# Turning quantised weights by DMA instead of on TensorE, in a one-core kernel of FFN, GRU and experts

## The chip, the cores and the metric

One core of a Trainium2 chip. The metric is the device time of one execution of the program in microseconds, as the median of several runs. The engines are PE (TensorE), DVE (VectorE), ACT (ScalarE), POOL (GpSimd) and SP (SyncE, which here only issues DMAs). Each runs its own instructions in order and waits for the others through semaphores.

## What is computed

```python
x = x + ffn0(cond0(x))        # x: 16 x 256 x 512, f32
x = x + experts1(gru1(x))

def ffn0(x):                  # microscaled ("MX") blocks of 32 along the last axis
    gate = q_act(x) @ q_w(w_gate).T        # w_gate, w_up: 2048 x 512
    up   = q_act(x) @ q_w(w_up).T
    return q_act(silu(gate) * up) @ q_w(w_down).T      # w_down: 512 x 2048

def q_w(w):                   # per block of 32: a shared power of two, then 1 mantissa bit, clipped at 6
    scale = 2 ** (floor(log2(max|w|)) - 2)
    return quantize_elem(w / scale, 2, 1.0, 6.0) * scale
```

cond0 sums blocks of 16 steps (x to 16 sums per batch row), forms keys, a softmax over the sums and a projection, adds it to x and normalises. gru1 is a GRU over the 256 steps, experts1 a linear layer with two of 16 low-rank experts per row. Only q_w of the three FFN weights, and where its result is put, is touched by the change.

## The kernel before

x is cut into 32 tiles of 128 rows (8 steps of 16 batch rows). A software pipeline goes over the tiles in slots, `slot(c, s)` with s from 0 to 7, one GRU step in each; FFN, GRU input products, GRU and experts work on different tiles in one slot. All but the first 170 us or so is this pipeline, and PE sets its pace.

Before it stands the weight stage. The three FFN weights are 24 pieces of 128 x 1024 f32 (512 KB). Each goes through five hands:
- SP loads it to `wst[u]`, u = p % 2 (L318; the second buffer is named `sg_gs` in the profile). It waits on `w_y` until POOL has scaled piece p-2 out of that buffer.
- DVE takes block maxima and makes scales from them (`scales`, L577 to L585), three pieces ahead of the rounding. The scales of piece k wait on `w_out` until piece k-4 is multiplied.
- POOL multiplies by the inverse scale (`scale_piece`, L989, output `gi`).
- ACT computes `absolute` (L420) and `summand` (L427), from which DVE rounds in two steps (L593, L595).
- POOL multiplies back (`piece`, L1002) into `wqn[u]`, bf16, which lies in `qfT`. It waits on `w_mm` until PE has turned piece p-2 out of that buffer.
- PE turns the piece in 8 blocks of 128 x 128 to PSUM (`ps_gate_up` or `ps_z`, L1083), and ACT copies it to its place in `wq` (`keep_piece`, L414).

POOL's order is scale 0, scale 1, then for each p: scale p+2, multiply back p. ACT's order for each p: keep p-1, absolute p+2, summand p+1. PE's order for each p: `block_sums(p)`, a step of `attention`, turn p. SP's order for each p: load p, then `beside(p)`: two or three of the 32 x tiles of 256 KB (until p = 12, in a ring of 8, each waits on `summed` for the tile 8 before), two small constants (p = 8 to 14), WkT and WoT (p = 13 and 15), chunks of W_hh (p = 18 to 21), the slots of c = -4 (from p = 21). The 10 steps of the attention (block sums to `proj`) stand one to a piece from p = 11 on, on every engine. From p = 21 on the slots of c = -4 stand between the pieces: `xs` (L1013), its statistics and normalisation.

After the last piece DVE takes maxima of W_hh (`chunk_max`, L698), PE turns them to a row (L1320), and the first FFN product (L1131) follows it.

Of the kernel before, what the change touches and what calls it, by code (L numbers as in the profile page):

```python
# [24 lines left out]
BF16 = mybir.dt.bfloat16  # L25
# [9 lines left out]
P = 128  # L35
# [19 lines left out]
PIECE = 1024  # L55
# [11 lines left out]
ROUND_UNIT = 2.0 ** 3  # L67
MOST_ROUND = (ROUND_UNIT * (255 + ROUND_LEAST)) ** 2
W_CLIP = 3.0
SCALED = 2.0 ** 13  # L70
LEAST = 2.0 ** -40
FILLS = 7
# [11 lines left out]
def wait(engine, sem, value):  # L84

    if value > 0:
        engine.wait_ge(sem, value)
# [11 lines left out]
def build(nc, x_steps, h0, ident, pick, block_mask, iota, rms_w, query, WkT, WoT, gamma, beta,  # L99
          ffn_w, W_ih, W_hh, b_ih, b_hh, WL, bias, rb1, rw2T, rb2, gates, BT, x1_dram, out):  # L100
    with ExitStack() as ctx:
# [3 lines left out]
        def sem(name):  # L105
            return ctx.enter_context(nc.semaphore(name))
# [133 lines left out]
        w_loaded = [sem(f"w_piece_loaded{u}") for u in range(2)]  # L240
        w_small, w_y, w_abs_ok = sem("w_scales"), sem("w_scaled"), sem("w_absolute")
        w_round_ok, w_added = sem("w_rounding_ready"), sem("w_rounding_added")
        w_q, w_out, w_mm, w_ev = sem("w_rounded"), sem("w_quantised"), sem("w_turned"), sem("w_kept")
        c_dve = sem("consts_computed")

        xin_loaded, xs_done, q_stat, ve_done, rstd_done = (
# [35 lines left out]
        def count_piece(turn, u, more=0):  # L282

            return turn * 2 + (u + more)
# [27 lines left out]
        @block.sync  # L312
        def _(sp):

            def piece(turn, u):
                wait(sp, w_y, count_piece(turn, u, -1))
                at = (turn * 2 + u) * P
                sp.dma_start(wst[u][:, :], ffn_w[at:at + P, :]).then_inc(w_loaded[u], 16)  # L318

            small = [(rw_b, rms_w.partition_broadcast(P)), (q_b, query.partition_broadcast(P)),  # L320
                     (maskA[:, :], block_mask), (iota_b[:, :], iota.partition_broadcast(P)),
                     (gamma_b[:, :], gamma.partition_broadcast(P)), (beta_b[:, :], beta.partition_broadcast(P)),
                     (bias_b[:, :], bias.partition_broadcast(P)), (b_i[:, :], b_ih), (b_h[:, :], b_hh),
                     (rb1_b[:, :], rb1.partition_broadcast(P)), (rb2_b[:, :], rb2[0:EXPERTS].partition_broadcast(P)),
                     (gates_b[:, :], gates.partition_broadcast(P)), (rw2_sb[:, :], rw2T)]
            assert len(small) == CONSTS

            def x_upto(p):

                if p < 0:  # L330
                    return 0
                return min(TILES, max(min(p + 1, 2) * XRING // 2, (p - 1) * TILES // SUM_PARTS))

            def beside(p):

                for t in range(x_upto(p - 1), x_upto(p)):
                    wait(sp, summed, t - XRING + 1)
                    sp.dma_start(xtile[t % XRING], x_steps[t * P:(t + 1) * P, :]).then_inc(xt_loaded[t % XRING], 16)
                if 8 <= p < 8 + (CONSTS + 1) // 2:
                    for dst, src in small[(p - 8) * 2:(p - 7) * 2]:  # L340
                        sp.dma_start(dst, src).then_inc(consts if p > 8 else att_consts, 16)
                if p == SUM_PARTS + 1:
                    sp.dma_start(wk_sb, WkT).then_inc(wkwo_loaded, 16)
                if p == SUM_PARTS + 3:
                    sp.dma_start(wo_sb, WoT).then_inc(wkwo_loaded, 16)
                    sp.dma_start(h[:, :], h0).then_inc(h0_loaded, 16)
                    load_x_in(0)
                k = p - FIRST_HOP - 7
                if 0 <= k < KD:
                    sp.wait_ge(at_pe, 2)  # L350
                    sp.dma_start(wih[:, k, :], W_hh[:, k, :]).then_inc(whh_loaded, 16)
                if p >= FIRST_SLOT:
                    slot(-4, p - FIRST_SLOT)

            def loads(c):
                Q, F, E, I, R, L = stages(c)
                if L:
                    wait(sp, x1b_done, count(c - 1, 1))
                    sp.wait_ge(x1_stored, count(c, 1) * 16)
                    sp.dma_start(x1_in[:, :], rows(x1_dram, c - 1)).then_inc(x1in_loaded, 16)  # L360
                if E:
                    wait(sp, x1_done, count(c + 2, 1))
                    sp.dma_start(xres[:, :], rows(x_steps, c + 2)).then_inc(xres_loaded, 16)

            def load_x_in(q):
                wait(sp, xs_done, count(q, 1))
                sp.dma_start(xin[:, :], rows(x_steps, q)).then_inc(xin_loaded, 16)

            def stores(c):
                Q, F, E, I, R, L = stages(c)  # L370
                if E:
                    sp.wait_ge(x1_done, count(c + 2, 1, 1))
                    sp.dma_start(rows(x1_dram, c + 2), x1[:, :]).then_inc(x1_stored, 16)
                if L:
                    sp.wait_ge(y_ok, count(c - 1, 1, 1))
                    sp.dma_start(rows(out, c - 1), y[:, :]).then_inc(y_stored, 16)

            def rows(dram, t):
                return dram[t * P:(t + 1) * P, :]

            def slot(c, s):
                if s == 0:
                    loads(c)
                if s == 4 and c + 5 < TILES:
                    load_x_in(c + 5)
                if c == -3 and s == STEPS - 2:
                    sp.dma_start(wl[:, 1:KD + 1, :], WL).then_inc(wl_loaded, 16)
                    for k in range(KD):
                        sp.wait_ge(whh_lo, min(k + 2, KD))
                        sp.dma_start(wih[:, k + 1, :], W_ih[:, k, :]).then_inc(wih_loaded, 16)  # L390
                    sp.dma_start(bt[:, :, :], BT).then_inc(bt_loaded, 16)
                if s == STEPS - 1:
                    stores(c)

            for p in range(PIECES):
                piece(p // 2, p % 2)
                beside(p)
            for s in range(PIECES - FIRST_SLOT, STEPS):
                slot(-4, s)
            over_tiles(slot)  # L400
            sp.wait_ge(y_stored, 16 * TILES)
            sp.wait_ge(x1_stored, 16 * TILES)
# [3 lines left out]
        def _(act):  # L406
            first = [(idf[:, :], ident), (pick_sb[:, 0:pick.shape[1]], pick)]
            for dst, src in first:
                act.dma_start(dst, src).then_inc(first_consts, 16)

            def keep_piece(turn, u):
                ps = (ps_up, ps_z)[u]
                act.wait_ge(w_mm, count_piece(turn, u, 1))
                nc.scalar.activation(wq[:, turn * 2 + u:turn * 2 + u + 1, :], ps[:, :].bitcast(BF16).unsqueeze(1),  # L414
                                     ACT.Copy).then_inc(w_ev, 1)

            def absolute(p):
                act.wait_ge(w_y, p + 1)
# [11 lines left out]
            def piece(turn, u):  # L430
                p = count_piece(turn, u)
                if p == 0:
                    absolute(0)
                    summand(0)
                    absolute(1)
                if p > 0:
                    keep_piece((p - 1) // 2, (p - 1) % 2)
                if p + 2 < PIECES:
                    absolute(p + 2)
                if p + 1 < PIECES:  # L440
                    summand(p + 1)
                if p == PIECES - 1:
                    keep_piece(turn, u)

            def attention(step):

# [519 lines left out]
        def _(pool):  # L966
# [25 lines left out]
            def piece(turn, u):  # L992

                p = count_piece(turn, u)
                if p + 2 < PIECES:
                    scale_piece(turn + 1, u)
                attention(p - FIRST_HOP)
                if p >= FIRST_SLOT:
                    slot(-4, p - FIRST_SLOT)
                pool.wait_ge(w_q, count_piece(turn, u, 1))  # L1000
                wait(pool, w_mm, count_piece(turn, u, -1))
                g.tensor_tensor(blocked(wqn[u]), blocked(wy[p % 3]), spread(wsc[p % 4][:, :]),  # L1002
                                ALU.mult).then_inc(w_out, 1)

# [60 lines left out]
        def _(pe):  # L1065
            mm, turn_ = nc.tensor.matmul, nc.tensor.transpose
            def block_sums(p):
# [3 lines left out]
                for t in range(p * TILES // SUM_PARTS, min((p + 1) * TILES // SUM_PARTS, TILES)):  # L1071
# [1 line left out]
                    first = (BLOCKS - 1 - t * BLOCKS // TILES) * B  # L1073
                    mm(ps_down[:, :], pick_sb[:, first:first + P], xtile[t % XRING], start=t == 0,
                       stop=t == TILES - 1).then_inc(summed, 1)

            def piece(turn, u):

                ps = (ps_up, ps_z)[u]
                wait(pe, w_ev, count_piece(turn, u, -1))  # L1080
                pe.wait_ge(w_out, count_piece(turn, u, 1))
                for m in range(PIECE // P):
                    last = turn_(ps[:, :].bitcast(BF16)[:, m * P:(m + 1) * P], wqn[u][:, m * P:(m + 1) * P], idb[:, :])  # L1083
                last.then_inc(w_mm, 1)

            def attention(step):
                if step == 1:
# [258 lines left out]
            for p in range(PIECES):  # L1346
                block_sums(p)
                attention(p - FIRST_HOP)
                piece(p // 2, p % 2)
            for s in range(STEPS):  # L1350
                slot(-4, s)
            pe.wait_ge(w_ev, PIECES)
            over_tiles(slot)


# [54 lines left out]
```

## Time and profile before

| | |
|---|---|
| time, median of 3 runs | 1749.04 us (1748.38 to 1749.63) |
| profiled execution | 1750.32 us, its span 1748.5 us |
| busy in the span | PE 1585.6 us (91%), DVE 1417.0 (81%), ACT 710.7 (41%), POOL 498.4 (29%) |
| DMA | 80.09 MB, mean 46 GB/s; 246, 265, 141, 111 GB/s in the first four of 40 slices |
| mean granted TensorE clock | 0.958 |

The span is from the first to the last instruction of the profiled execution. The table's shares are means over the whole span, and most of it is the pipeline; the weight stage is its first three slices (43.7 us each). So the views below are cut to the first 170 us. PE, DVE and so on are the engines' own busy time; "idle before <- releaser" is what an engine waited for before an instruction. Numbers like 1.00 under PEclk are the granted TensorE clock as a share of 2.4 GHz.

### The profile page before, as it was taken

How to read it: one execution, taken by the hardware profiler on the slowest of the kernel's cores; microseconds unless marked ns; L12 is line 12 of the kernel's file. 1: busy time of each engine (PE TensorE's matmuls, PEld its weight loads, DVE VectorE, ACT ScalarE, POOL GpSimd, SP SyncE). 2: the span in 40 equal slices, each digit the busy share in tenths (PEclk: the TensorE clock that was granted, in tenths of full speed). 3: DMA queues.
4: the chain of work that ended last, by engine and by line, in shares of the span. 5: the costliest groups of instructions: out<-in, count | busy, mean ns of one | idle time of the engine just before them, and what ended most of it. 6: DMA issues, size and time to landing. Idle time of an engine off the chain costs nothing.

```text
span 1748.5 us, 76340 instructions
## 1 busy us (share of the span) xinstructions
PE 1585.6 (91%) x32908; PEld 1240.8 (71%) x32908; DVE 1417.0 (81%) x5579; ACT 710.7 (41%) x1760; POOL 498.4 (29%) x573
## 2 busy tenths in 40 slices
PE   5534489999999999999999999999999999999986
PEld 2221167777787877778777777877777777778874
DVE  7898888888888888888888888888888888887654
ACT  5653244444444344434344434443443444443331
POOL 6773232222222222222222222222222222221100
PEclk9855699999999999999999999999999999999998
DMA  7733100011001010001111000110100010000000
GB/s 246 265 141 111 43 26 27 34 33 33 13 29 33 33 33 33 29 31 34 33 33 34 33 26 16 33 33 33 33 33 27 33 33 33 27 27 27 21 15 20
DMA packets 35408, 80.09 MB, mean 46 GB/s; under 512 B 4864, under 2 KB 5248, under 8 KB 34688
## 3 DMA queue, kind: packets, MB, share of 16 engines
q1 hardware_dynamic: 34784, 75.03, 12.6%
q8 instruction: 259, 4.24, 1.1%
q14 instruction: 77, 0.63, 0.1%
q10 hardware_dynamic: 288, 0.19, 0.0%
HBM read 58.43 MB, written 16.78 MB: 43 GB/s over the span
## 4 chain that ended last, share of the span: by engine, by line
PE 76%; DVE 16%; issue 2%; DMA 2%; POOL 2%; ACT 1%; DVEq 0%; ACTq 0%; POOLq 0%; SPq 0%
PE ps_rn_turn L1305 23%; PE ps_gi L1198 11%; PE ps_z L1305 10%; PE ps_gate_up L1137 6%; PE ps_down L1155 6%; PE ps_gate_up L1131 4%; PE ps_base L1207 4%; PE ps_base L1251 3%; PE ps_route L1207 3%; DVE fe L795 1%; PE ps_rn_turn L1146 1%; PE ps_rn_turn L1175 1%; DVE gi L595 1%; DVE gi L593 1%; DVE zn L780 1%
## 5 line engine op out<-in xcount | busy, mean ns | idle before, releaser
L1305 PE MATMUL ps_rn_turn<-hT,whh 128*128 128x32 f16 x16320 | 449.2, 176 | 39.2 <-DVE hT L733 38.8
L1305 PEld LDWEIGHTS ps_rn_turn<-hT,whh 128*128 128x128 f16 x16320 | 435.0, 96 | 65.7 <-DVE hT L733 58.2
L1020 POOL TENSOR_TENSOR qf<-f8c,fe 128x512 bf16<-128x512 bf16 x128 | 135.6, 1059 | 892.4 <-DVE f8c L812 872.8
L1198 PE MATMUL ps_gi<-x1T,wih 128*128 128x128 f16 x4608 | 288.6, 219 | 1.2 <-ACT gi L544 1.2
L1198 PEld LDWEIGHTS ps_gi<-x1T,wih 128*128 128x128 f16 x4608 | 270.3, 98 | 25.6 <-issue 1.5
L553 ACT ACTIVATE r_tanh<-r_pre,scale_half 128x64 f32<-128x64 f32 x256 | 89.0, 348 | 461.5 <-DVE r_pre L753 461.5
L1305 PE MATMUL ps_z<-hT,whh 128*128 128x32 f16 x8160 | 243.3, 176 | 0.0
L1305 PEld LDWEIGHTS ps_z<-hT,whh 128*128 128x128 f16 x8160 | 222.7, 96 | 0.0
L544 ACT ACTIVATE gi<-ps_gi,b_i,scale_x 128x128 f32<-128x128 f32 x384 | 144.7, 457 | 181.9 <-PE ps_gi L1198 181.9
L747 DVE TENSOR_TENSOR r_half<-ps_rn_turn,gi 128x64 f32<-128x64 f32 x256 | 56.6, 221 | 137.6 <-PE ps_rn_turn L1305 134.4
L555 ACT ACTIVATE z_tanh<-z_pre,scale_half 128x64 f32<-128x64 f32 x256 | 89.0, 348 | 157.9 <-DVE z_pre L763 157.9
L1131 PE MATMUL ps_gate_up<-wq,qxT 128*128 128x512 bf16 x512 | 135.5, 388 | 12.8 <-DVE inter L827 12.8
L1137 PE MATMUL ps_gate_up<-wq,qxT 128*128 128x512 bf16 x512 | 139.1, 396 | 2.4 <-ACT sg_gs L504 2.4
L1155 PE MATMUL ps_down<-wq,qfT 128*128 128x512 bf16 x512 | 134.4, 386 | 0.0
L557 ACT ACTIVATE n<-n_pre,scale_half 128x64 f32<-128x64 f32 x256 | 89.0, 348 | 20.6 <-DVE n_pre L770 10.5
L1207 PE MATMUL ps_base<-wl,hT 128*128 128x512 f16 x384 | 94.3, 382 | 0.0
L827 DVE TENSOR_TENSOR inter<-ps_gate_up,sg_gs 128x512 f32<-128x512 f32 x128 | 87.4, 683 | 7.1 <-PE ps_gate_up L1137 7.1
L504 ACT ACTIVATE sg_gs<-ps_gate_up 128x512 f32<-128x512 f32 x128 | 74.2, 580 | 44.5 <-PE ps_gate_up L1131 44.5
L788 DVE TENSOR_REDUCE fam<-inter 128x16 f32<-128x512 f32 x128 | 87.9, 686 | 4.4
L806 DVE SCALAR_TENSOR_TENSOR f<-inter,finv 128x512 fp8e4<-128x512 f32 x128 | 87.7, 685 | 0.0
L1155 PEld LDWEIGHTS ps_down<-wq,qfT 128*128 128x128 bf16 x512 | 48.6, 100 | 49.9 <-issue 4.6
L1137 PEld LDWEIGHTS ps_gate_up<-wq,qxT 128*128 128x128 bf16 x512 | 43.3, 99 | 55.6 <-issue 20.9
(197 smaller groups left out, 2590.1 us busy)
## 6 DMA issues: line engine op xcount, KB each, us to landing
wih<-in_x_steps SPq DMA_DIRECT2D x32, 256.0 KB, 5.4
xin<-in_x_steps SPq DMA_DIRECT2D x32, 256.0 KB, 3.5
xres<-in_x_steps SPq DMA_DIRECT2D x32, 256.0 KB, 3.1
x_dram<-x SPq DMA_DIRECT2D x32, 256.0 KB, 2.1
x_in<-x_dram SPq DMA_DIRECT2D x32, 256.0 KB, 2.8
out_rows<-y SPq DMA_DIRECT2D x32, 256.0 KB, 2.0
wst<-in_ffn_w SPq DMA_DIRECT2D x12, 512.0 KB, 3.7
sg_gs<-in_ffn_w SPq DMA_DIRECT2D x12, 512.0 KB, 3.9
```

The lines of the kernel that those rows point to most:

```text
L544: last = nc.scalar.activation(gi_gate(i, g)[:, k, :], ps_gi[:, k * P:(k + 1) * P], ACT.Identity, bias=b_i[:, g * KD + k:g * KD + k + 1], s ...
L553: nc.scalar.activation(r_tanh[:, :], r_pre[:, :], ACT.Tanh, scale=HALF_S_INV).then_inc(r_ok, 1)
L555: nc.scalar.activation(z_tanh[:, :], z_pre[:, :], ACT.Tanh, scale=HALF_S_INV).then_inc(z_ok, 1)
L557: nc.scalar.activation(n[:, :], n_pre[:, :], ACT.Tanh, scale=HALF_S_INV).then_inc(n_ok, 1)
L788: v.tensor_reduce(am[:, :], blocked(src[:, :]), AX_X, ALU.max, apply_absolute_value=True).then_inc(small, 1)
L1020: g.tensor_tensor(blocked(qf[:, :]), blocked(f8c[:, :]), spread(fe16[:, :]), ALU.mult).then_inc(qf_done, 1)
L1131: last = mm(ps_gate[:, :], qxT[:, k, :], w_ffn(0, n, k), start=k == 0, stop=k == KD - 1)
L1137: last = mm(ps_up[:, :], qxT[:, k, :], w_ffn(8, n, k), start=k == 0, stop=k == KD - 1)
L1155: last = mm(ps_down[:, :], qfT[:, i, :], w_down(i), start=i == 0, stop=i == NF * KD - 1)
L1198: last = mm(ps_gi[:, j * P:(j + 1) * P], wih_parts[:, k, at:at + P], x1T[:, x, k, :], start=k + w + x == 0, stop=k == KD - 1 and w == 1)
L1207: last = mm(out, hT[l % 2][:, 2 * k + x, :], wl_parts[:, k, begin:begin + n], start=k + w + x == 0, stop=stop and w == 1)
L1305: last = mm(ps[:, (at + j) * 2 * B:(at + j + 1) * 2 * B], whh[:, k, u, gate * D + j * P:gate * D + (j + 1) * P], hx(t)[:, 2 * k:2 * k + 2, ...
```

## The change

The turns on PE and the copies on ACT are left out. Instead SP issues one DMA transpose for each piece, from `wqn[p % 2]` to `wq[:, p, :]`, both in SBUF: the 8 blocks of 128 x 128 are turned on the way. The turn of piece p-5 stands in `beside(p)`, behind the load of piece p and ahead of the x tiles and constants; it waits on `w_out` until POOL has multiplied that piece back, which at that place is already so. The last five turns stand behind the loop over the pieces. POOL's wait for the buffer and PE's wait before the pipeline are now on the turns' own semaphores, one for each parity of pieces.

```diff
@@ constants
+LATER = 5
@@ SP
+            def turn_piece(p):
+
+                sp.wait_ge(w_out, p + 1)
+                sp.dma_start_transpose(wq[:, p, :].rearrange("p (m n) -> p m n", n=P), wqn[p % 2]).then_inc(
+                    w_turned[p % 2], 16)
+
             def beside(p):
 
+                if p >= LATER:
+                    turn_piece(p - LATER)
                 for t in range(x_upto(p - 1), x_upto(p)):
...
             for p in range(PIECES):
                 piece(p // 2, p % 2)
                 beside(p)
+            for p in range(PIECES - LATER, PIECES):
+                turn_piece(p)
             for s in range(PIECES - FIRST_SLOT, STEPS):
                 slot(-4, s)
@@ ACT
-            def keep_piece(turn, u):
-                ps = (ps_up, ps_z)[u]
-                act.wait_ge(w_mm, count_piece(turn, u, 1))
-                nc.scalar.activation(wq[:, turn * 2 + u:turn * 2 + u + 1, :], ps[:, :].bitcast(BF16).unsqueeze(1),
-                                     ACT.Copy).then_inc(w_ev, 1)
...
-                if p > 0:
-                    keep_piece((p - 1) // 2, (p - 1) % 2)
                 if p + 2 < PIECES:
                     absolute(p + 2)
                 if p + 1 < PIECES:
                     summand(p + 1)
-                if p == PIECES - 1:
-                    keep_piece(turn, u)
@@ POOL, piece
                 pool.wait_ge(w_q, count_piece(turn, u, 1))
-                wait(pool, w_mm, count_piece(turn, u, -1))
+                wait(pool, w_turned[u], 16 * turn)
                 g.tensor_tensor(blocked(wqn[u]), blocked(wy[p % 3]), spread(wsc[p % 4][:, :]),
                                 ALU.mult).then_inc(w_out, 1)
@@ PE
-            def piece(turn, u):
-
-                ps = (ps_up, ps_z)[u]
-                wait(pe, w_ev, count_piece(turn, u, -1))
-                pe.wait_ge(w_out, count_piece(turn, u, 1))
-                for m in range(PIECE // P):
-                    last = turn_(ps[:, :].bitcast(BF16)[:, m * P:(m + 1) * P], wqn[u][:, m * P:(m + 1) * P], idb[:, :])
-                last.then_inc(w_mm, 1)
...
             for p in range(PIECES):
                 block_sums(p)
                 attention(p - FIRST_HOP)
-                piece(p // 2, p % 2)
             for s in range(STEPS):
                 slot(-4, s)
-            pe.wait_ge(w_ev, PIECES)
+            for u in range(2):
+                pe.wait_ge(w_turned[u], 16 * TURNS)
             over_tiles(slot)
```

## Rows read from the trace of the kernel before

**Rows 1.** Busy time by stretch; PEclk, DMA share and GB/s stand last.

```profile
0.00:30.00 30.00, 14.29 (x44) 6.45 (x44) 18.70 (x33) 13.56 (x13) 17.87 (x20) 1.00 0.67 235
30.00:72.00 42.00, 28.34 (x122) 13.77 (x120) 33.47 (x49) 27.39 (x28) 32.52 (x18) 0.92 0.90 295
72.00:137.00 65.00, 23.06 (x126) 14.60 (x124) 58.65 (x87) 36.48 (x40) 48.87 (x30) 0.63 0.39 139
```

**Rows 2.** Chain that ended last, 114 to 146 us: start, us, what.

```profile
116.12 1.01 PE ps_z L1083 x8
117.13 5.00 PE ps_base L1114 x8
...
122.71 0.84 issue
...
143.27 1.01 PE ps_route L1320 x4
```

**Rows 3.** DVE's waits, 0 to 137 us: us in total, times, longest.

```profile
DVE ps_gi L577 <- DMA wst<-in_ffn_w: 5.5, 2, 3.1
DVE ps_gi L577 <- DMA sg_gs<-in_ffn_w: 5.2, 3, 2.1
DVE gi L593 <- ACT ps_rn_turn L427: 3.9, 8, 0.9
DVE stats L904 <- POOL xs L1013: 1.5, 1, 1.5
```

**Rows 4.** DVE in order of time: start, us, line; idle before it last.

```profile
45.55 1.23 DVE L577 TENSOR_REDUCE ps_gi<-sg_gs 128x32 f32<-128x1024 f32 x1 [1.76 <-DMA sg_gs<-in_ffn_w]
...
72.05 1.23 DVE L577 TENSOR_REDUCE ps_gi<-wst 128x32 f32<-128x1024 f32 x1 [3.06 <-DMA wst<-in_ffn_w]
...
83.02 1.22 DVE L593 SCALAR_TENSOR_TENSOR gi<-gi,ps_rn_turn 128x1024 f32<-128x1024 f32 x1 [0.43 <-ACT ps_rn_turn L427]
...
125.66 1.22 DVE L593 SCALAR_TENSOR_TENSOR gi<-gi,ps_rn_turn 128x1024 f32<-128x1024 f32 x1 [0.55 <-ACT ps_rn_turn L427]
```

**Rows 5.** Groups by line, 0 to 150 us: busy us, mean ns | idle before.

```profile
L1002 POOL TENSOR_TENSOR qfT<-gi,wsc 128x1024 bf16<-128x1024 f32 x24 | 46.1, 1921 | 15.0 <-DVE gi L595 15.0
...
L414 ACT ACTIVATE wq<-ps_z 128x1024 bf16<-128x1024 bf16 x12 | 12.3, 1024 | 17.3 <-PE ps_z L1083 17.3
...
L1083 PE MATMUL ps_z<-idb,qfT 128*128 128x128 bf16 x96 | 9.7, 262 | 31.3 <-POOL qfT L1002 31.3
```

**Rows 6.** SyncE in order of time: loads 9, 14 and 16.

```profile
39.22 0.33 SPq L318 DMA_DIRECT2D sg_gs<-in_ffn_w  x1
...
64.33 0.33 SPq L318 DMA_DIRECT2D wst<-in_ffn_w  x1
...
76.23 0.33 SPq L318 DMA_DIRECT2D wst<-in_ffn_w  x1
```

**Rows 7.** GpSimd in order of time: scale 9, multiply back 7 and 13.

```profile
47.48 1.91 POOL L989 TENSOR_TENSOR gi<-sg_gs,winv 128x1024 f32<-128x1024 f32 x1 [1.70 <-DVE wsc L585]
49.80 1.91 POOL L1002 TENSOR_TENSOR qfT<-gi,wsc 128x1024 bf16<-128x1024 f32 x1 [0.40 <-DVE gi L595]
...
80.97 1.91 POOL L1002 TENSOR_TENSOR qfT<-gi,wsc 128x1024 bf16<-128x1024 f32 x1 [0.18 <-DVE gi L595]
```

**Rows 8.** DMA issues, KB, median us to landing; the last: 72 to 137 us.

```profile
wih<-in_x_steps SPq DMA_DIRECT2D x32, 256.0 KB, 5.4
...
out_rows<-y SPq DMA_DIRECT2D x32, 256.0 KB, 2.0
...
beta_b<-in_beta SPq DMA_DIRECT2D x1, 256.0 KB, 8.8
...
wst<-in_ffn_w SPq DMA_DIRECT2D x4, 512.0 KB, 3.3
```

**Rows 9.** PE in order of time: block sums at either level of the clock.

```profile
46.38 2.79 PE L1074 MATMUL ps_down<-wih,inter 128*128 128x512 f32 x6
...
52.66 4.04 PE L1074 MATMUL ps_down<-wih,inter 128*128 128x512 f32 x6
```

More of the change, by code:

```diff
@@ L242, in build @@
         w_round_ok, w_added = sem("w_rounding_ready"), sem("w_rounding_added")
-        w_q, w_out, w_mm, w_ev = sem("w_rounded"), sem("w_quantised"), sem("w_turned"), sem("w_kept")
+        w_q, w_out, w_turned = sem("w_rounded"), sem("w_quantised"), [sem(f"w_turned{u}") for u in range(2)]
         c_dve = sem("consts_computed")
```

## The prediction, made before the changed kernel had run

> **What bounds the kernel now.** I read the busy time by stretch first. The change touches only the first 137 us, in which 24 weight pieces are quantised and turned; the other 1600 us keep their instructions. Three stretches differ there [rows 1]. From 30 to 72 us the DMA engines are busy 0.90 of the time at 295 GB/s, VectorE (DVE) 33.5 of 42 us. From 72 to 137 us DMA is down to 0.39 and DVE is busy 58.7 of 65 us. So DVE is the bound after 72 us, and before it DVE shares that place with the loads.
>
> Then DVE's waits, since whatever DVE doesn't wait for is covered [rows 3]: 10.7 us for loaded pieces, 3.9 us for ScalarE (ACT) at L427, 1.5 us for `xs` of GpSimd (POOL). PE isn't among them. The timeline shows when: the waits for loads stand at 45.6 and 72.1 us (and at 56.2), those for ACT are under a microsecond each [rows 4]. Last the chain of waits: it passes through the turns of PE and the copies of ACT where these hold up what stands behind them, as at 116.12 to 123.56 us, where a turn goes ahead of the projection L1114 and a copy ahead of `absolute` [rows 2].
>
> **What is removed.** Per piece 8 PE turns, about 0.6 to 1.0 us, and one ACT copy of 1.02 us, 24.6 us of ACT over 24 pieces [rows 5]. Nearly all lies beside DVE. What counts is DVE's wait for L427, 3.9 us in eight waits. I attribute 3.1 of them to the copy that stands ahead of `absolute` and `summand`; the last, 0.8 us at 129.4 us, is the time of L427 itself and stays. Of the 3.1 us, 1.7 fall before 72 us, ahead of a wait for a load that ends at a time of its own. I count these as nothing there, for the load is late next. After 72 us there are 0.43 (83.0 us), 0.43 (120.2) and 0.55 (125.7) [rows 4], and L1114 can start 1.0 us sooner, of which GpSimd's order (xs stands behind `scale_piece(23)`, which ends at 122.04) lets through 0.85. Together -2.2 us. Bounds: 0 if DVE merely finds the next wait, -4.0 if all 3.1 + 0.85 come home.
>
> **What is added to the DMA engines.** 24 transfers of 256 KB from SBUF to SBUF. The trace has no transfer that turns, so the price X of one on the rings is bounded. As plain bytes: the stretch of 30 to 72 us moved 295 GB/s at a share of 0.90, so 328 GB/s when busy, and 262,144 bytes take 0.80 us [rows 1]. From above, the longest landing of any 256 KB transfer here is 8.8 us (`beta_b`) [rows 8]; it includes its queue. From below, a transfer that needs no HBM read may fit into gaps of a ring that waits for HBM: 0. I take 0.80, since the x tiles and weight loads of the same stretch are moved by the same queue in the same direction.
> The Trainium skill (DMA: Bandwidth & Descriptors, Latency and other measured facts) has turning DMAs at 261 GB/s in one measured case and 350 to 400 in the contiguous one; no run here shows either. By that X would be an estimated 1.0 or 0.7 us, and the sum below 1.4 us more or 0.7 less.
>
> Where do they fall? SyncE issues `turn_piece(p-5)` right behind the load of piece p. In the full stretch these are pieces 4 to 10 behind loads 9 to 15, issued at 39.22 to 68.61 us (first and others in [rows 6]). There load 9 took 39.22 to 45.55 us, and load 14 from 64.33 to 72.05 us, and DVE stood waiting 1.8 and 3.1 us [rows 4, 6]. Seven times 0.80 is 5.6 us of ring time ahead of loads that are late already. At the low end two more turns (0 to 3 fall in part before) and the idle 0.10 x 42 = 4.2 us set against each other give 9 x 0.80 - 4.2 = 3.0 us.
>
> **The wait that is added.** GpSimd's `piece(p)` now waits for the turn of p-2 to have landed, where it waited for PE's (long done). That turn is issued behind load p+3, which SyncE issues once `scale_piece(p+1)` is done. Between them GpSimd does `piece(p-1)` and `scale_piece(p+2)`, some 4.4 us. In the quiet stretch: load 16 is issued at 76.23 us, and GpSimd multiplies piece 13 at 80.97 us [rows 6, 7], so the turn of piece 11 has 4.7 us from the issue of the load. Loads land there in 3.3 to 3.4 us [rows 8], and 0.80 more is 4.2: it fits, by half a microsecond. Cost 0; bounds 0 to +1 (X up to 1.4). Queued behind a late turn would be L1002, the next `scale_piece`, then ACT's `absolute` and DVE.
> In the full stretch it doesn't fit. Behind load 9 the turn of piece 4 lands at 45.55 + 0.80 = 46.35 us; L1002 of piece 6 and `scale_piece(9)` follow with 2 x 1.99, so L989 ends at 50.3 instead of 49.4 [rows 7]: 0.9 us. There are three such loads (9, 11, 14), so 0 to 2.6 us; much of it overlaps with the longer landing already counted, and I take one, 0.9.
>
> **What is added to SyncE.** The turn's issue stands ahead of x tiles, constants and W_hh. Load issues take 0.33 to 0.43 us here, a turn's is unknown; SyncE waits 76.6 us for L989 in this stage, so 24 issues of up to 2 us still fit. The x tiles then come later by that time, which only block sums see; their reader `br` (ACT, 70.6 us) stands beside DVE's wait for load 14, cover of 3 us. Five turns now stand at the end ahead of `load_x_in(1)`, once issued at 124.19 us and now about 136; the pace is set by POOL there (xs at 137.3 us), so up to 1.5 us of a GpSimd step that DVE doesn't need before chunk_max ends at 142.9 us. I count 0. PE now waits for all turns before its first FFN product: piece 23 is multiplied by 134.8 us, its turn lands by 139, PE is due at 144.28, behind 143.27 [rows 2]. Hidden, with 5 us of cover.
> **PE's clock.** The granted clock is 0.92 in 30 to 72 us and 0.63 after [rows 1]. If an emptier PE ran block sums at the lower level, six records would take 4.0 instead of 2.8 us [rows 9]; DVE doesn't wait for them. L1114 shows 5.0 us, 0.6 per record, already the slow one. Cost 0.
>
> **The sum.** -2.2 + 5.6 + 0.9 = +4.3 us. Against the profiled execution, 1750.3 us, that is 1754.6; that execution was 1.3 us above the median, and on the median of 1749.0 it gives **1753.3 us**. A measurement of this kernel can tell about 0.2%, 3.5 us, from no change.
>
> **Rivals.**
> - *The turns are hidden* (not slower). A source in SBUF needs no HBM read: `out_rows`, SBUF to HBM and 256 KB, lands in 2.0 us, where the same bytes as an x tile need 5.4 [rows 8]. If turns slip into the gaps, nothing is added and -2.2 to -4.0 us remain: 1745 to 1747 us. Against it: the share of 0.90 leaves few gaps. It decides when X on the rings is under 0.3 us, for seven of these are 2.1 us. Chance 22%.
> - *Turning is slow on the rings* (X of 1.5 to 3 us; small runs, or elements of 2 bytes written one by one). At X = 2.0: 7 x 2.0 = 14, the quiet stretch misses its 4.7 us by 0.7 and, as two periods share one such wait, pays 0.3 on 11 pieces, 3.8; with -2.2 and 0.9 that is +16: 1765 us. At 3.0 it is 21 + 0.8 x 11 + 0.9 - 2.2 = +28: 1777. Chance 15%.
> - *Turning paces the stage.* From X = 2.8 on (a load of 512 KB takes 1.6 us of the rings, a piece 4.4) each piece takes 1.6 + X. At the 8.8 us of `beta_b` [rows 8], 22 pieces x 10.4 + 30 - 137 = +122: 1871 us. Chance 4%, the `beta_b` landing being mostly queue. The Trainium skill (VectorE: DVE Perf Modes, The three transpose paths) gives a 128x128 block by DMA 1309 ns, against 390 on TensorE; the same page's eight blocks one after another would be an estimated 10.5 us a piece and +159 us by the same working. That is the rule that speaks against the change most; the trace has no turn to test it by.
> - *The forecast's mechanism*, contention in the full stretch and small gains after it, 0 to +10 us: 59%.
>
> **How the numbers follow.** Of the forecast's 59%, 41 lie above +3.5 us and 18 within. Of the hidden case's 22%, 12 are within and 10 faster. The two slow cases, 19%, are slower. So faster 0.10, within 0.30, slower 0.60. The range goes from 1746 (all but the best of the hidden case) to 1775 us (most of the slow one), and leaves out some 15%.
>
> **What would show it.** In the profile after: DVE's waits for loads grow from 10.7 to about 17 us, all before 75 us; its wait for L427 falls from 3.9 to about 1; GpSimd's L1002 waits for the turns in the stretch of 30 to 72 us and hardly after 76; the turns land 4 to 5 us after their issue in the quiet stretch, 7 in the full one; the DMA share of 30 to 72 us goes towards 1; chunk_max (L698) starts at about 140.5 instead of 136.2 us; and the time from there to the end is unchanged. It is wrong if the turns raise the DMA share by far more than 0.8 us each, if DVE waits for ACT as before, or if PE's first L1131 waits for `w_turned`.

## The result and the profile after

| | before | after |
|---|---|---|
| median, 19 runs each | 1749.95 us | 1753.51 us |
| ratio to before, 95% interval | | 1.0018 (1.0011 to 1.0025) |
| profiled execution, its span | 1750.32, 1748.5 us | 1750.73, 1748.9 us |
| start of `chunk_max` (end of the weight stage) | 136.1 us | 138.5 us |

The change makes the kernel 3 us slower (0.18%), just inside the 0.2% that the prediction calls no change. The median was forecast as 1753.3. The baseline of that forecast was 1749.04 us, from three runs; over all 19 runs it is 1749.95. As a difference, +4.3 us was forecast, and +3.1 (by the ratio) to +3.6 (by the medians) was measured.

Where the stage ends, `chunk_max` on DVE, is a sharper mark than the whole time: from there to the end of the span it took 1610 to 1614 us in all profiles below, with no order in it that follows the changes. The mark isn't exact either: the changed kernel profiled once more had it at 136.9 us, 1.6 us sooner. A difference of under some 1.5 us between two marks shows nothing by itself.

Busy time by stretch, after, answers to [rows 1]; columns as there:

```profile
0.00:30.00 30.00, 12.33 (x19) 5.07 (x20) 19.53 (x33) 10.70 (x10) 17.63 (x20) 0.81 0.72 228
30.00:72.00 42.00, 29.20 (x46) 10.40 (x44) 33.07 (x49) 18.05 (x18) 30.89 (x17) 0.73 1.08 341
72.00:137.00 65.00, 16.99 (x32) 7.95 (x32) 57.63 (x82) 25.34 (x29) 49.99 (x30) 0.56 0.75 201
```

The rings' share now reads 1.08 in the full stretch (above one, so it is an index and no fraction), and they move 341 GB/s where before it was 295 at 0.90. ACT has 9.3 us less to do in that stretch and 11.1 in the next. The granted clock of PE is lower in both, but how much lower differs from profile to profile: the same kernel profiled once more had 0.84 and 0.60 where this one has 0.73 and 0.56.

The waits of 0 to 140 us, after, answer to [rows 3]: us in total, times, longest.

```profile
ACT w_abs L425 <- POOL gi L990: 63.7, 22, 7.1
...
POOL qfT L1003 <- DMA wq<-qfT: 15.0, 13, 4.2
...
DVE ps_gi L578 <- DMA wst<-in_ffn_w: 6.6, 5, 3.1
...
DVE gi L594 <- ACT ps_rn_turn L432: 4.5, 8, 0.9
DVE ps_gi L578 <- DMA sg_gs<-in_ffn_w: 3.6, 4, 1.3
```

DVE's waits for loads did not grow: 10.2 us, where they were 10.7. New is GpSimd's wait for turns, 15.0 us in 13 waits. And DVE waits for ACT as long as before, though the copies are gone (4.5 us, where it was 3.9). That was a sign by which the prediction called itself wrong. ACT waits for GpSimd's scaling, which stands behind the product that waits for the turn. The 63.7 us of that wait are not the sign: in the kernel without turns below they are 59.7, with DVE waiting for ACT only 1.9 us. What counts is that a late product makes the next scaling late. GpSimd in order of time shows it, with the load and the turn that SyncE issued before it (answering to [rows 6, 7]):

```profile
42.77 1.91 POOL L990 TENSOR_TENSOR gi<-wst,winv 128x1024 f32<-128x1024 f32 x1
47.43 1.91 POOL L1003 TENSOR_TENSOR qfT<-gi,wsc 128x1024 bf16<-128x1024 f32 x1 [2.74 <-DMA wq<-qfT]
49.42 1.91 POOL L990 TENSOR_TENSOR gi<-sg_gs,winv 128x1024 f32<-128x1024 f32 x1
```

```profile
40.43 0.33 SPq L319 DMA_DIRECT2D sg_gs<-in_ffn_w  x1
40.80 1.23 SPq L338 DMA_TRANSPOSE wq<-qfT  x1
42.07 2.23 SPq L347 DMA_DIRECT2D wih<-in_x_steps  x3
```

Load 9 goes out at 40.43, the turn of piece 4 behind it at 40.80, and product 6 on GpSimd starts at 47.43, 6.6 us after that issue. `scale_piece(9)` follows it and ends at 51.3 us, where the prediction had 50.3 and the kernel before 49.4.

The DMA issues by stretch: KB, median us to landing. First 30 to 72 us, then 72 to 137 us, both after:

```profile
wih<-in_x_steps SPq DMA_DIRECT2D x19, 256.0 KB, 5.1
sg_gs<-in_ffn_w SPq DMA_DIRECT2D x5, 512.0 KB, 5.1
...
wq<-qfT SPq DMA_TRANSPOSE x9, 5.8
```

```profile
wst<-in_ffn_w SPq DMA_DIRECT2D x4, 512.0 KB, 3.8
...
wq<-qfT SPq DMA_TRANSPOSE x13, 4.4
```

### The profile page after: what moved, and what is told of

It reads as the page before. It is cut to its first block, busy times and chain, and to the rows that moved or that the text cites. A ratio compares the mean times of both kernels' runs of the same rounds, so it can differ in the third digit from the quotient of the medians.

```text
span 1748.9 us, 75935 instructions
## 1 busy us (share of the span) xinstructions
PE 1577.8 (90%) x32716; PEld 1229.0 (70%) x32716; DVE 1416.0 (81%) x5579; ACT 687.4 (39%) x1736; POOL 499.2 (29%) x573
## 2 busy tenths in 40 slices
DMA packets 60750, 86.35 MB, mean 49 GB/s; under 512 B 30208, under 2 KB 30592, under 8 KB 60032
## 4 chain that ended last, share of the span: by engine, by line
PE 76%; DVE 15%; DMA 2%; issue 2%; POOL 2%; ACT 1%; SPq 0%; DVEq 0%; ACTq 0%; POOLq 0%
PE ps_rn_turn L1297 23%; PE ps_gi L1190 11%; PE ps_z L1297 10%; PE ps_gate_up L1129 6%; PE ps_down L1147 6%; PE ps_gate_up L1123 4%; PE ps_base L1199 4%; PE ps_base L1243 3%; PE ps_route L1199 3%; DVE fe L796 1%; PE ps_rn_turn L1138 1%; PE ps_rn_turn L1167 1%; DMA wih<-in_x_steps 1%; POOL gi L990 1%; DVE hT L783 1%
## 5 line engine op out<-in xcount | busy, mean ns | idle before, releaser
L1147 PE MATMUL ps_down<-wq,qfT 128*128 128x512 bf16 x512 | 133.8, 384 | 0.0
L558 ACT ACTIVATE n<-n_pre,scale_half 128x64 f32<-128x64 f32 x256 | 89.0, 348 | 20.4 <-DVE n_pre L771 10.5
L1147 PEld LDWEIGHTS ps_down<-wq,qfT 128*128 128x128 bf16 x512 | 48.4, 99 | 49.4 <-issue 3.9
```

The lines of the kernel that those rows point to most:

```text
L558: nc.scalar.activation(n[:, :], n_pre[:, :], ACT.Tanh, scale=HALF_S_INV).then_inc(n_ok, 1)
L1147: last = mm(ps_down[:, :], qfT[:, i, :], w_down(i), start=i == 0, stop=i == NF * KD - 1)
```

## The experiments

The ratios are to the kernel before on the same chip, of all comparable runs. "Mark" is the start of `chunk_max` in the profile.

| kernel | ratio (95% interval) | mark, us |
|---|---|---|
| before | 1 | 136.1 |
| changed, first and second | 1.0018 (1.0011 to 1.0025), 1.0014 (1.0005 to 1.0023) | 138.5, 136.9 |
| no turns | 0.9989 (0.9980 to 0.9998) | 133.9 |
| PE turns kept, DMA turns added | 1.0022 (1.0013 to 1.0031) | 138.9 |
| four buffers | 0.9995 (0.9986 to 1.0004) | 134.5 |
| four buffers and a copy more | 1.0030 (1.0019 to 1.0041) | 140.4 |
| PE turns kept, unused | 1.0026 (1.0017 to 1.0035) | 138.2 |
| turn ahead of the load | 0.9998 (0.9988 to 1.0008) | 134.6 |
| copy in place of turn | 1.0020 (1.0011 to 1.0030) | 138.7 |
| LATER = 6 | 1.0383 (1.0367 to 1.0399) | 202.2 |
| LATER = 4 | 1.0035 (1.0022 to 1.0047) | 141.3 |
| DMA turns from piece 12 on | 0.9995 (0.9986 to 1.0005) | 133.8 |
| the same, turn ahead of the load | 0.9998 (0.9989 to 1.0007) | 132.9 |

### The removal alone

```diff
-                sp.wait_ge(w_out, p + 1)
-                sp.dma_start_transpose(...)
+                return
@@ POOL, piece
-                wait(pool, w_turned[u], 16 * turn)
-                g.tensor_tensor(blocked(wqn[u]), ...
+                g.tensor_tensor(blocked(wq[:, p, :]), ...
```

> The removal alone: no turn by anyone. GpSimd writes each piece unturned straight into wq, so the FFN works on unturned weights; PE waits for the last piece itself. Measured against before. My sum priced the removal at -2.2 us (bounds 0 and -4.0), DVE's chunk_max would start near 134.0 us instead of 136.2, and DVE's wait for ACT would fall from 3.9 to about 1 us. Rival (the clock): with PE emptier its granted clock falls in the stage, the projection (L1106 of after) takes 6.4 us as in after instead of 5.2, and of the 2.2 us about 1 is left. A third view, that the trace of after still shows 4.5 us of DVE waiting for ACT and so the copy never was its cause, would give 0.

Measured 0.9989, -1.9 us (the interval is -3.5 to -0.3), and the mark at 133.9 us. DVE's wait for ACT fell to 1.9 us. The term of -2.2 us holds, and the view that the copy never was the cause falls: the 4.5 us in the profile after must come from something else. The projection (L1114 before, L1106 in the changed kernel) took 5.3 us, not 6.4, so an emptier PE doesn't by itself make it long.

### The addition alone

```diff
@@ kernel before, SP
+            def turn_piece(p):
+                sp.wait_ge(w_out, p + 1)
+                wait(sp, w_turned[p % 2], 16 * (p // 2))
+                sp.dma_start_transpose(spare[p % 2]..., wqn[p % 2]).then_inc(w_turned[p % 2], 16)
...
+                if p >= LATER:
+                    turn_piece(p - LATER)
@@ POOL, piece
                 wait(pool, w_mm, count_piece(turn, u, -1))
+                wait(pool, w_turned[u], 16 * turn)
```

> The addition alone: the kernel before with its PE turns and ACT copies, and besides each piece is turned by DMA into a spare buffer, at the place and with the GpSimd wait of the changed kernel. Measured against before. My sum: +5.6 for the rings and +0.9 for the wait, +6.5 us, chunk_max near 142.7 us, and DVE's waits for loads 6 us longer. Rival (the cost is GpSimd's wait for the turn, as the trace of after suggests, and ring time alone costs little): +3 to +5 us, with DVE's waits for loads near 10 us as before. If the clock were what costs in after, the addition alone would cost under 1 us, since PE stays as full as before.

1.0022, +3.9 us (+2.3 to +5.4), mark at 138.9 us. That is below the 6.5 us of my sum and what the view of GpSimd's wait gave. The waits of DVE and GpSimd in this kernel:

```profile
POOL qfT L1017 <- DMA hT<-qfT: 16.5, 12, 3.7
...
DVE ps_gi L591 <- DMA wst<-in_ffn_w: 6.1, 3, 3.4
...
DVE ps_gi L591 <- DMA sg_gs<-in_ffn_w: 3.8, 4, 1.3
```

Loads cost DVE 9.9 us, no more than before; turns cost GpSimd 16.5. With -1.9 for the removal the two add up to +2.0 us, within the intervals of the changed kernel's +2.4 and +3.1.

### The wait or the rings: four buffers

```diff
         wqn = [qfT_flat[:, u * PIECE:(u + 1) * PIECE] for u in range(2)]
+        wqn += [tile[:, :, :].rearrange("p k n -> p (k n)").bitcast(BF16) for tile in hT]
@@ POOL, piece
-                wait(pool, w_turned[u], 16 * turn)
+                wait(pool, w_turned[p % 4], 16 * (p // 4))
```

> The changed kernel with four buffers instead of two between GpSimd and the turns (the two new ones lie in hT, unused in this stage), so GpSimd waits for the turn of piece p-4 and not p-2. Ring traffic and PE are as in the changed kernel. If GpSimd's wait carries the cost, its 15.0 us of waiting for turns go to nearly 0, chunk_max starts at 135 to 136 us instead of 138.6, and the time is 2 to 3 us below the changed kernel, about that of before. If the ring time carries it (my sum: 5.6 of 6.5), the time stays within 1 us of the changed kernel, +3 us against before, and DVE's waits for loads grow instead.

0.9995 and 134.5 us. In this kernel no wait of GpSimd for a turn is left among its waits, and the cost is gone: 4.0 us below the changed kernel by the first ratio, 3.3 by the second. It moves every byte that the changed kernel moves. Against the kernel without turns, 24 turns cost 0.6 us of the mark and 1.0 us by the ratios, both within what these measurements can tell from nothing. Its stretch of 30 to 72 us:

```profile
30.00:72.00 42.00, 29.10 (x49) 10.82 (x48) 33.92 (x51) 18.99 (x19) 32.52 (x17) 0.78 1.10 361
```

361 GB/s instead of 295 over 42 us are 2.8 MB more: about nine turns (2.4 MB) and what the stage is ahead.

### Is there room for more?

```diff
@@ four buffers, behind each turn
+                wait(sp, w_again[p % 4], 16 * (p // 4))
+                sp.dma_start(spare[p % 4], wqn[p % 4]).then_inc(w_again[p % 4], 16)
```

> Four buffers, and besides each turn a plain copy of the same 256 KB from SBUF to a spare SBUF tile: ring time once more, without GpSimd waiting for it soon. With one turn a piece the stage is 0.6 us longer than with none (134.5 against 133.9 us at chunk_max). If the rings really have room in the stretch of 30 to 72 us (the share of 0.90 being mostly waiting for HBM), chunk_max moves by 1 us or less again. If they were full and one turn just fitted in, the second transfer costs 0.8 us on some 7 to 9 pieces: +5 to +7 us, chunk_max at 140 to 141 us, and DVE's waits for loads grow by as much.

1.0030 and 140.4 us: 5.9 us behind four buffers alone. DVE's waits for loads grew to 17.6 us, from 10.8 with four buffers:

```profile
DVE ps_gi L584 <- DMA wst<-in_ffn_w: 9.8, 7, 4.0
...
DVE ps_gi L584 <- DMA sg_gs<-in_ffn_w: 7.8, 5, 2.3
```

Product 13 on GpSimd starts at 86.3 us, where it was 79.6, so the loss arises before the quiet stretch. The rate of 30 to 72 us stayed where it was, so in this mixture of transfers it had no more to give:

```profile
30.00:72.00 42.00, 29.16 (x44) 10.11 (x42) 31.68 (x48) 16.51 (x16) 29.82 (x17) 0.72 1.10 360
```

The first 256 KB a piece were moved on top of the loads. The second cost what my prediction charged for the first.

### Is it the turning, or any transfer there?

```diff
-                sp.dma_start_transpose(wq[:, p, :].rearrange("p (m n) -> p m n", n=P), wqn[p % 2]).then_inc(
-                    w_turned[p % 2], 16)
+                sp.dma_start(wq[:, p, :], wqn[p % 2]).then_inc(w_turned[p % 2], 16)
```

> The changed kernel with a plain SBUF-to-SBUF DMA copy in the place of each turn, so the FFN works on unturned weights; all waits are the same. It prices turning against copying. If a turn is plain bytes on the rings, as my X of 0.80 us had it, GpSimd waits for landings as long as now (15 us) and chunk_max starts at 138 to 139 us. If turning itself is longer (a turn lands a median 4.4 us after its issue in the quiet stretch, of which 1.23 us is SyncE's own time where a copy's issue takes 0.4), copies land 1 to 1.5 us sooner, the waits fall to 5 us or less, and chunk_max starts at 135 to 136 us.

1.0020 and 138.7 us, as the changed kernel. GpSimd waited 12.8 us for the copies, which land in 5.8 us (median) in the full stretch and 3.9 in the next, where turns land in 5.8 and 4.4. So in time a turn costs what plain bytes cost, to within half a microsecond of landing. SyncE is held 1.23 us by its issue and 0.47 by a copy's, and as the time is the same, the longer issue isn't the cost either.

On the rings a turn is more than plain bytes, though. This is SyncE's queue in the whole kernel, before, after and with copies: packets, MB, and the time of the packets as a share of 16 engines' span.

```profile
q1 hardware_dynamic: 34784, 75.03, 12.6%
```

```profile
q1 hardware_dynamic: 60128, 81.32, 14.6%
```

```profile
q1 hardware_dynamic: 38240, 81.32, 13.6%
```

The same 6.3 MB take 2.0% of the span (35 us, an estimated 1.5 us a turn) as turns and 1.0% (17 us, 0.7 a copy) as copies. By stretch the share is 1.08 and 0.75 with turns, 0.98 and 0.59 with copies, at nearly the same GB/s (341 and 201, 325 and 205). The doubled share cost no time in this place, which says again that the share of the rings isn't what the changed kernel pays for.

### Where the turn is issued

First ahead of the load:

```diff
             for p in range(PIECES):
+                if p >= LATER:
+                    turn_piece(p - LATER)
                 piece(p // 2, p % 2)
                 beside(p)
```

> The changed kernel with one move: SyncE issues the turn of piece p-5 ahead of the load of piece p and not behind it, so it waits for GpSimd's product only (which is done 2 us before the scaling that the load waits for), and its packets don't queue behind 512 KB. Same buffers, same bytes, same PE. If the cost is the landing of the turn behind the load, GpSimd's 15.0 us of waits for turns fall under 3, chunk_max starts near 134.5 us as with four buffers (138.5 in the changed kernel), and the time is 1 us below before (3 to 5 us below the changed kernel). If the turn's own length is what counts, most of the 15.0 us stay and chunk_max stays past 137 us. If loads suffer from a turn ahead of them, DVE's waits for loads grow from 10 to 15 us.

0.9998 and 134.6 us, 2.8 to 3.5 us below the changed kernel, with its two buffers and its bytes. GpSimd waited 3.6 us, of which the longest wait is one of 2.2. Loads cost DVE 11.9 us, hardly more. It is level with before and not 1 us below, but the interval of 0.9988 to 1.0008 can't tell one from the other.

Then one piece later:

```diff
-LATER = 5
+LATER = 6
```

> The changed kernel with LATER = 6: the turn of piece p-2, for which GpSimd waits before piece p, now stands behind the load of p+4, which waits for the scaling p+2, directly ahead of that product on GpSimd. Nothing of GpSimd's work covers it any more. Theory of GpSimd's wait: a piece takes 0.4 (load issue) + 4.4 to 5.8 (landing of the turn) + 2 x 1.99 = 8.8 to 10 us instead of 4.4 to 5, on some 17 pieces: +65 to +90 us. If ring time were the cost, the place of the issue would hardly matter: +3 us as in the changed kernel.

The time is 67 us longer than before, at the lower end of what the theory of GpSimd's wait expected; GpSimd waits for turns 17 times, 84.4 us in all. The time of a piece can be read off GpSimd:

```profile
74.48 1.91 POOL L1003 TENSOR_TENSOR qfT<-gi,wsc 128x1024 bf16<-128x1024 f32 x1 [4.98 <-DMA wq<-qfT]
76.47 1.91 POOL L990 TENSOR_TENSOR gi<-wst,winv 128x1024 f32<-128x1024 f32 x1
83.81 1.91 POOL L1003 TENSOR_TENSOR qfT<-gi,wsc 128x1024 bf16<-128x1024 f32 x1 [5.42 <-DMA wq<-qfT]
```

From product to product it takes 8.9 to 10.0 us between 65 and 103 us: two instructions of GpSimd, 1.99 us each with their gaps, and 5.0 to 6.1 of waiting. The same transfers, one load later, cost twenty times as much.

And one piece sooner:

```diff
-LATER = 5
+LATER = 4
```

> The changed kernel with LATER = 4: SyncE issues the turn of p-4 behind the load of p, and so waits for GpSimd's product (2 us) ahead of the x tiles; the turn that GpSimd needs is issued some 2.4 us sooner than with 5. If GpSimd's wait for the landing is the cost, its 15.0 us of waits fall to 3 or less and chunk_max starts at 134.5 to 135.5 us, as with the turn ahead of the load; time 3 to 4 us below the changed kernel. If holding up the x tiles behind a waiting SyncE costs as much, block sums end later, DVE's waits for loads grow past 13 us, and chunk_max stays past 137 us.

A miss: 1.0035 and 141.3 us. GpSimd's waits for turns did go, none is left among its waits, but DVE's waits for loads rose to 19.7 us, the longest 6.6. SyncE in order of time shows a queue of its own making:

```profile
67.83 0.43 SPq L352 DMA_DIRECT2D wih<-in_WkT  x1
68.31 0.43 SPq L319 DMA_DIRECT2D wst<-in_ffn_w  x1
68.78 1.96 SPq L338 DMA_TRANSPOSE wq<-qfT  x1
70.79 3.94 SPq L350 DMA_DIRECT2D rw_sb<-in_rw2T  x1
74.78 0.57 SPq L319 DMA_DIRECT2D sg_gs<-in_ffn_w  x1
```

While SyncE waits for GpSimd's product, the x tiles and constants behind it are held up, and then stand ahead of the next load: load 14 goes out at 68.31 us, directly behind 1 MB of WkT, and load 15 at 74.78, behind the issue of a 4 KB constant that held SyncE for 3.94 us (0.99 with 5). With 5 the two loads were at 66.43 and 70.46, load 14 behind WkT there too. The second half of that expectation, the rival, is what happened.

### The clock

```diff
@@ changed kernel: PE turns put back, no ACT copy
+                wait(pool, w_mm, count_piece(turn, u, -1))
...
+                piece(p // 2, p % 2)
```

> The changed kernel with the PE turns put back, their results unused (no ACT copies). This fills PE as before. Clock theory: the granted clock of 30 to 72 us is back near 0.92 (0.73 in the changed kernel), the projection takes 5.2 us again instead of 6.4, and chunk_max starts 1.2 us or more earlier than in the changed kernel, minus up to 1.0 us for the turn that stands ahead of the projection; net 0 to -1 us. If x tiles and block sums at the higher clock matter in the full stretch too, -2 us. If the clock doesn't matter, +1 us against the changed kernel.

The clock of 30 to 72 us was 0.84. That is 0.73 in the first profile of the changed kernel, but 0.84 in its second, which has no turn on PE, so the fuller PE isn't shown to have raised it. The projection took 5.3 us, and yet the mark is only 0.3 us earlier, inside its uncertainty, and the time is 1.0026. So a fuller PE does not take the loss away. The four buffers say the same from the other side: at a clock of 0.78 and with a projection of 6.6 us there is no loss (0.9995). The clock isn't its cause. On the projection alone the clock does act. The granted clock of two microseconds in its middle, first before, then after:

```profile
120.00:122.00 2.00, 2.00 (x6) 0.71 (x5) 1.78 (x2) 0.15 (x1) 1.92 (x2) 0.99 0.00 0
```

```profile
122.00:124.00 2.00, 2.00 (x4) 0.69 (x3) 1.61 (x4) 0.74 (x1) 1.92 (x2) 0.50 0.00 0
```

The projection began at 116.9 and 118.7 us. Before, it had the full clock from about 120 us on, 3 us after its start; after, 122 to 124 us is still at the low level and 124 to 126 shows 0.95, with the projection's end at 125.1: 5.2 against 6.4 us on the chain. (0.50 and 1.00 are 1.2 and 2.4 GHz.) In the profiles of the ten kernels with no turn on PE beside it, it took anything from 5.1 us (turn ahead of the load) to 6.6 us (copy in place of turn), and 6.0 us when the changed kernel was profiled again. What decides between them I didn't find.

### The full stretch or the quiet one

```diff
+BY_DMA = 12        # pieces 0 to 11 on PE and ACT as before, the others by DMA
```

> Pieces 0 to 11 are turned on PE and copied on ACT as before, pieces 12 to 23 by DMA as in the changed kernel (behind the load of piece p+5, two buffers). No turn is on the rings before load 17 (about 81 us). If the loss of the changed kernel arises in the full stretch alone, product 13 on GpSimd starts at 81.0 us as before, and with the copies gone after it chunk_max starts at 134.5 to 135.5 us: 0.5 to 1.5 us below before. If GpSimd's wait costs in the quiet stretch too, or PE's clock takes the gain (the projection at 6.4 instead of 5.2 us), chunk_max starts at 136 us or later, no change against before.

The mark is at 133.8 us, product 13 on GpSimd starts at 79.2 us instead of 81.0, and GpSimd waits 1.2 us for turns. The time is 0.9995. So the loss doesn't arise in the quiet stretch; it is one of the full stretch. How much was gained this profile can't say: product 13 was expected at 81.0 us, as nothing about turning changes ahead of it, and 1.8 of the 2.3 us by which the mark is earlier lie there. From product 13 to the mark it takes 54.6 us, before 55.2, in the changed kernel 54.8 and without turns 53.6; the last difference is mostly the projection, 6.0 us here and 5.3 there. The second kernel of this kind issues the turn ahead of the load:

> A version built from what the runs showed: pieces 0 to 11 on PE and ACT as before, pieces 12 to 23 by DMA, each turn issued ahead of the load and not behind it. GpSimd's waits for turns, 1.2 us in the run of pieces 12 to 23 alone, go to 0; chunk_max starts at 133.3 to 134 us and the time is 1 to 2.5 us below before, near the run without any turns (0.9989). If it is not below before by 1 us, the last microsecond of GpSimd's wait was not on the path, and what the copies gave back is at its end.

The mark is the earliest of all, 132.9 us, and no wait for a turn is left. But the time is 0.9998: its pipeline happened to take 1614 us from the mark to the end of the span, the longest in these profiles. The expectation of 1 to 2.5 us below before was missed, and with an interval of 0.9989 to 1.0007 this run can't say whether anything was gained. No version that turns the weights is measurably faster than the kernel before; the most that these runs leave to be had is the 1.9 us of no turns at all.

The changed kernel once more:

> The changed kernel as it is, once more, beside the two below, to see how far a stage's end in one profile can be trusted. If it can, chunk_max starts within 0.5 us of 138.5 us and the ratio to before is 1.001 to 1.0025.

1.0014 confirms the sign and size; the mark at 136.9 us missed its 0.5 us and shows how far one profile can be trusted.

## Why the prediction was right, and where it wasn't

The time was right to 0.2 us on the median, and that is luck. Two terms of the sum were wrong, one each way, and the baseline of 1749.04 us was 0.9 below the median of all runs. The measured terms are -1.9 for the removal, 0.6 to 1.0 for the transfers and 3.3 to 4.0 for GpSimd's wait: +2.0 to +3.1, where -2.2 + 5.6 + 0.9 = +4.3 was forecast.

- **Removed, -2.2 us**: -1.9 us measured by the kernel without turns. Right in total. That most of it lies behind 72 us fits as well, as far as one profile shows: product 13 starts 0.7 us sooner than before, the mark 2.3 us.
- **The price X of a turn, 0.80 us, as plain bytes**: right in what it costs, wrong on the rings. A copy in its place changes nothing in the time, and a second transfer of the size (a plain copy) costs 5.9 us of the mark where 7 x 0.80 = 5.6 was the sum. But the turns take an estimated 1.5 us of the rings each, the copies 0.7. "The turns raise the DMA share by far more than 0.8 us each" was one of the signs of being wrong, and it came. By X = 1.5 the same sum would have been 4.9 us higher, and further off.
- **Ring time of seven turns, +5.6 us**: the step that failed. I read a DMA share of 0.90 [rows 1] as full and charged every byte. With four buffers the stretch took nine turns by going from 295 to 361 GB/s, for 0.6 us of the mark. The lower bound, 3.0 us, was too high as well: setting 0.10 x 42 us of idle time against the turns takes the share for a measure of room, and it isn't one. The rival "hidden" came nearer, as the turns went in beside the loads; it failed by overlooking the wait. Its reason, that the rings wait for HBM and a source in SBUF doesn't, fits but isn't shown: no run put another read from HBM in the place of the turns.
- **GpSimd's wait, +0.9 us**: the mechanism was right and its size wrong. Four buffers take away that wait alone and give back 3.3 to 4.0 us. I had counted it for the three loads that were late. In fact GpSimd waited in eight places of the full stretch (8.9 us) and 4.2 us more for product 11 at 74.6 us, since behind the loads there the turn lands after 5.8 us (median) and GpSimd's cover is 4.4. And it hit ACT and DVE because ACT's `absolute` stands right behind `scale_piece`: I had noted the queue and not that it has no slack (ACT waits for the scaling 22 times).
- **The quiet stretch, cost 0**: right. The turns landed in 4.4 us against a cover of 4.7, three waits of 0.3 to 0.7 us; DMA turns from piece 12 on alone left the time level with before (0.9995).
- **SyncE**: issues of 1.23 us fit. The turns at the end hold up `load_x_in(1)` until 138.4 us, and GpSimd waits 1.6 us for it beside `chunk_max`; hidden, as said.
- **PE's clock, cost 0**: half right. Block sums don't matter: DVE doesn't wait for them, and with four buffers there is no loss at a clock of 0.78. But I misread two rows. The block sums of 4.0 us [rows 9] and the projection's 5.0 us weren't at the lower level: the clock was 0.68 on average over the former, and the projection had the full clock in its last 2 us. So it could still become slower, and took 1.2 us longer in the changed kernel's profile, on the chain. That it isn't the loss is shown; how much of the single profile's 2.4 us it is, is not.
- **What would show it**: the DMA share near 1, the landings in the quiet stretch and the waits in the full one were right. DVE's waits for loads (17 us forecast, 10.2 seen), its wait for ACT (1 forecast, 4.5 seen) and `chunk_max` (140.5 forecast, 138.5 and 136.9 seen) were not. These are just the rows that tell ring time from GpSimd's wait. Of the three signs of being wrong two came: DVE waited for ACT as before, and the turns raised the share by more than 0.8 us each. PE's first product of the FFN did not wait for `w_turned`.

The chances put 0.60 on slower by over 0.2% and 0.30 on no change. The loss of 0.14 to 0.18% is real, but lies inside that bound, so the case with 0.30 happened.

## What to carry to other kernels

When a step is moved to a DMA, ask first who must see it landed before reusing its source, and count from the issue of whatever stands ahead of it in the same queue: here a kernel with the same bytes is level with the one before when it has two more buffers or issues them ahead of the load, 3 us slower when they stand behind it, and 67 us one load later. A busy share of 0.90 of the DMA engines on loads from HBM didn't say that an SBUF-to-SBUF transfer finds no room; the rate in GB/s, and a second transfer beside the first, did. And a wait put on a queue (LATER = 4) moves the wait to everything behind it.

## What the runs showed of the hardware that I had not expected

- Transfers from SBUF to SBUF went in beside HBM loads at a share of 0.90: 295 to 361 GB/s with four buffers, the loads landing in 5.3 and 6.1 us (`sg_gs` and `wst`, medians of the full stretch) where before it was 5.4 and 5.6. In the quiet stretch the loads of the changed kernel land later, in 4.3 and 3.8 us instead of 3.4 and 3.3. The share reads 1.08 to 1.10 with turns, and stays there when more is queued, and 0.98 with copies in their place.
- A DMA transpose of 128 x 1024 bf16 takes 1.23 us of SyncE (up to 2.6 in the full stretch) and lands in a median of 4.4 us behind a load in the quiet stretch, 3.3 us ahead of it; as a plain copy behind the load, 3.9 us. It moves small packets: those under 512 B rose from 4,864 to 30,208 in the whole kernel, with copies only to 5,248. Its share of the rings is twice that of a copy. The Trainium skill (DMA: Bandwidth & Descriptors, Latency and other measured facts) has turning DMAs at 261 GB/s in the one measured case and at 350 to 400 in the contiguous one. No run here shows a rate for turns alone; against copies the difference was half a microsecond of landing in the quiet stretch, twice the share of the rings, and none of the time. The 1309 ns for a block of 128 x 128 (the Trainium skill, VectorE: DVE Perf Modes, The three transpose paths) aren't the pace of blocks one after another here: eight of them would be an estimated 10.5 us, and the eight of a piece landed in 4.4, or in 3.0 at the least.
